# Norms fused into the feed-forwards, a delta rule with stacked fp32r parts, and grouped attention in two row halves

## The reference

```python
x = x + attn_causal_16_heads(norm(x))      # at1: head size 128
x = x + ffn_ternary(norm(x))               # ff2: silu(gate) * up, RMS norm, down; 1024 wide
x = x + delta_rule(norm(x))                # dr3: 16 heads of 16, 64 chunks of 16 tokens
x = x + ffn_ternary(norm(x))               # ff4
x = x + attn_grouped(norm(x))              # ga5: 32 query heads of 8, 8 key heads, not causal
x = x + ffn_hadamard(norm(x))              # ff6
x = x + attn_alibi_causal(norm(x))         # at7
x = x + ffn_hadamard(norm(x))              # ff8

# delta rule, per head, chunk by chunk (kc, vc: 16 x 16)
z = kc @ W
W = W - kc.T @ ((z - vc) * 2 / 256)
```

## Time and profile before

| | |
|---|---|
| median of 3 runs | 4026.34 us (4024.76 to 4029.02) |
| the profiled execution, its own time | 4044.84 us |
| its span | 4043.0 us |
| mean granted clock of TensorE | 0.955 |
| busy: PE, DVE, ACT, POOL | 3636.1, 2522.9, 1987.3, 762.7 us |

### The profile page before, as it was taken

How to read it: one execution, slowest core, us unless ns; L and a number is a source line. 1 busy time by engine, 2 the same in 40 slices (tenths; PEclk the granted TensorE clock), 3 DMA queues, 4 the chain that set the end, 5 groups by cost and what they waited for, 6 DMA issues and landing times. The chain is left out here.

```text
span 4043.0 us, 55040 instructions
## 1 busy us (share of the span) xinstructions
PE 3636.1 (90%) x19935; PEld 2559.5 (63%) x20020; DVE 2522.9 (62%) x4918; ACT 1987.3 (49%) x4137; POOL 762.7 (19%) x832
## 2 busy tenths in 40 slices
PE   6999999999387997867999999969799999999989
PEld 5878788787275986731333333248677777777767
DVE  5656566565653664537888888634576666666643
ACT  3555555554342332414777777722355555555532
POOL 1000000000131441310000000030144434444410
PEclk9999999999698997977999999989899999999999
DMA  1000000000000000011000000020000000000000
GB/s 51 11 7 11 11 5 11 11 5 2 32 1 20 1 0 3 1 44 44 20 16 17 17 16 17 1 80 1 22 8 11 11 5 11 11 7 9 2 32 22
DMA packets 32929, 61.42 MB, mean 15 GB/s; under 512 B 7186, under 2 KB 21522, under 8 KB 30842
## 3 DMA queue, kind: packets, MB, share of 16 engines
q1 hardware_dynamic: 32682, 58.12, 4.6%
HBM read 48.53 MB, written 9.18 MB: 14 GB/s over the span
## 5 line engine op out<-in xcount | busy, mean ns | idle before, releaser
L1495 DVE TENSOR_REDUCE ga5m_nm<-ga5m_M 128x1 f32<-128x1024 f32 x512 | 605.9, 1221 | 126.5 <-PE ga5m_M L1398 124.6
L1483 ACT ACTIVATE ga5m_pr<-ga5m_E 128x512 f32<-128x512 f32 x1024 | 558.5, 599 | 231.7 <-PE ga5m_E L1434 214.9
L376 PE MATMUL at_A<-at_pT,at_V 128*128 128x512 f32 (+3 forms) x1536 | 519.2, 488 | 7.4 <-issue 5.1
L319 POOL TENSOR_TENSOR at_prob<-at_prob,at_slope_row 128x128 f32<-128x128 f32 (+7 forms) x256 | 370.1, 1449 | 577.0 <-DVE at_prob L570 576.4
L376 PEld LDWEIGHTS at_A<-at_pT,at_V 128*128 128x128 f32 x1536 | 283.9, 190 | 248.7 <-issue 204.4
L464 ACT ACTIVATE at_pT<-at_T 128x512 f32<-128x512 f32 (+3 forms) x768 | 347.5, 488 | 107.2 <-PE at_T L417 105.9
L1398 PE MATMUL ga5m_M<-ga5m_K,ga5m_Q 128*128 128x512 bf16 x978 | 303.4, 389 | 61.4 <-DMA ga5m_Q<-in_zrows 38.9
L417 PE MATMUL at_T<-all_ident,at_prob 128*128 128x128 f32 x2304 | 336.4, 273 | 9.1 <-ACT at_pT L464 9.0
L1434 PE MATMUL ga5m_E<-ga5m_Q,ga5m_K 128*128 128x512 bf16 x986 | 336.1, 382 | 4.1 <-ACT ga5m_pr L1483 2.6
L1434 PEld LDWEIGHTS ga5m_E<-ga5m_Q,ga5m_K 128*128 128x128 bf16 x1024 | 98.9, 97 | 302.8 <-ACT ga5m_pr L1483 221.5
L417 PEld LDWEIGHTS at_T<-all_ident,at_prob 128*128 128x128 f32 x2304 | 268.1, 140 | 31.7 <-issue 8.9
(11 more groups left out here) (289 smaller groups left out, 8523.9 us busy)
## 6 DMA issues: line engine op xcount, KB each, us to landing
ga5m_Q<-ga_qs SPq DMA_DIRECT2D x96, 96.0 KB
at_raw_qk<-in_pqk SPq DMA_DIRECT2D x32, 256.0 KB, 2.8
at_raw_v<-in_pv SPq DMA_DIRECT2D x16, 256.0 KB, 3.1
at_raw_o<-in_po SPq DMA_DIRECT2D x32, 128.0 KB, 2.0
ga_qs<-ga5s_part SPq DMA_DIRECT2D x6, 512.0 KB
ga5m_K<-ga_ks SPq DMA_DIRECT2D x48, 48.0 KB
all_X<-in_x SPq DMA_DIRECT2D x1, 2048.0 KB
tq_raw<-in_gu SPq DMA_DIRECT2D x1, 2048.0 KB, 8.0
```

The lines of the kernel that those rows point to most:

```text
L319: nc.gpsimd.tensor_tensor(dst[:, 0:end], dst[:, 0:end], slope_row[n // 2 % 2][:, 0:end], ALU.add).then_inc(ramp_done, 1)
L376: mm = nc.tensor.matmul(bank[:, lo:GQ * P], V[b][:, kt, col:col + DH], pT[g][:, kt, lo:GQ * P], start=(kt == 0), stop=(kt == GQ * (g + 1) ...
L1483: nc.scalar.activation(pr[e % NR][:, :], Eb[e % 3][:, :], ACT.Exp, scale=scale).then_inc(e_done, 1)
L1495: nc.vector.tensor_reduce(nm[half % 2][:, m:m + 1], Mb[v % 2][:, :], AX.X, ALU.max, negate=True).then_inc(m_free[v % 2], 1)
```

## The change

Three parts. **Norms**: ff2, ff4 and ff6 also make the norm of the layer behind them (`nxt`), group by group as x is finished, so that `layer_norm` ahead of dr3, ga5 and at7 goes; the weights of dr3 and ga5 are fetched during ff2 and ff4 (`fetch`). **Delta rule**: one block dr3p makes rotary keys, values and turned keys, splits both into two fp32r parts and stores them; the stacks `KS` and `KVS`, which hold on 48 rows (3 x 16) high, low, high against high, high, low of one chunk, are read back from HBM by DMA, so that a product contracts over a chunk alone, in fp32r, and `MK` and its 256 ACT operations go. **Grouped attention**: two fp32r parts in place of three bf16 ones, stacks of 32 + 2 rows, held twice, in partitions 0 to 63 and 64 to 127. The two matmuls of an M use one half each, and successive E alternate between them.

```diff
 # normed_swiglu
+        if fetch:
+            @block.sync
+            def _(sp):
+                for tile, source, sem in fetch:
+                    sp.dma_start(tile, source).then_inc(sem, 16)
...
                     gate_up(g, f)
+                    if nxt is not None and f == 0 and g >= 2:
+                        turn_next(g - 2)
...
+            if nxt is not None:
+                turn_next(NG - 2)
             down(NG - 1, 0)
...
-                    if f == 0 and g:
+                    if f == 1 and g:
                         inverse(g - 1)
+                if nxt is not None and f == 5 and g:
+                    next_root(g - 1)
...
 # delta_rule
+        def load_stacks(sp, t, b):
+            rows = slice((b * QT + t) * P, (b * QT + t + 1) * P)
+            for i in range(3):
+                part = kvs[i == 1][rows, 0:D].rearrange("(j s) n -> s j n", s=C)
+                sp.dma_start(KS[b][C * i:C * i + C, :, :].bitcast(F32), part).then_inc(s_in[b], 16)
+                part = kvs[i == 2][rows, :].rearrange("(j s) n -> s j n", s=C)
...
+                for t in range(1, QT):
+                    for b in range(BATCH):
+                        sp.wait_ge(pp_done, (t - 1) * NP + (b + 1) * DC * PC)
+                        load_stacks(sp, t, b)
...
-                        mm = nc.tensor.matmul(PP[p % 2][:, e, :, :], MK[q % 2][:, 2 * pair + e, :],
-                                              KV[:, bass.ds(t + b * QT, 1), c, :, :].rearrange("p a v n -> p (a v n)"),
-                                              start=True, stop=True)
+                        mm = nc.tensor.matmul(PP[p % 2][:, e, :, :], KS[b][:, 2 * pair + e, c * P:(c + 1) * P],
+                                              KVS[b][:, 2 * pair + e, :, c, :], start=True, stop=True)
...
 # grouped_attention
-                    for lo in range(0, SEQ, 512):
-                        mm = nc.tensor.matmul(Mb[v % 2][:, lo:lo + 512], Q[n % NSLOT][:, x:x + P],
-                                              K[n % NSLOT][:, lo:lo + 512], start=True, stop=True)
+                    for half in range(2):
+                        lo = half * 512
+                        mm = nc.tensor.matmul(Mb[v % 2][:, lo:lo + 512], Q[n % NSLOT][rows(half), x:x + P],
+                                              K[n % NSLOT][rows(half), lo:lo + 512], start=True, stop=True)
...
-                    nc.tensor.matmul(Eb[e % 3][:, :], K[n % NSLOT][:, kt * P:(kt + 1) * P],
-                                     Q[n % NSLOT][:, x:x + 512], start=True, stop=True).then_inc(s_done, 1)
+                    nc.tensor.matmul(Eb[e % 3][:, :], K[n % NSLOT][rows(e % 2), kt * P:(kt + 1) * P],
+                                     Q[n % NSLOT][rows(e % 2), x:x + 512], start=True, stop=True
+                                     ).then_inc(s_done, 1)
```

More of the change, by code:

```diff
@@ L734, in turn @@
                         pe.wait_ge(ms_done, g - 1)
+                if nxt is not None and g >= 3:
+                    pe.wait_ge(next_done, (g - 2) * DC)
                 pe.wait_ge(xn_done, (g + 1) * GT)
@@ L774, in square_sums @@
                 pe.wait_ge(acc_done, (g + 1) * (FC - 1))
+                if nxt is not None and g:
+                    pe.wait_ge(next_done, g * DC)
                 if g + 1 < NG:
@@ L799, in _ @@
             down(NG - 1, 1)
+            if nxt is not None:
+                turn_next(NG - 1)
         @block.scalar
@@ L818, in high, with copy_next @@
                     nc.scalar.activation(sq[F % 2][:, :], hf[F % 2][:, :], ACT.Square).then_inc(sq_done, 1)
+            def copy_next(g):
+                for c in range(DC):
+                    act.wait_ge(nturn_done, g * DC + c + 1)
+                    nc.scalar.activation(nxt[0][:, c, g * N:(g + 1) * N], turned[c][:, :], ACT.Copy
+                                         ).then_inc(ncopy_done, 1)
             copy_turned(0)
@@ L828, in _ @@
                     high((F - 1) // FC, (F - 1) % FC)
+                if nxt is not None and f == 1 and g >= 2:
+                    copy_next(g - 2)
                 if f == 5 and g + 1 < NG:
@@ L946, in _ @@
                     low(F - 1)
+                if nxt is not None and len(nxt) == 2 and f == 1 and g >= 2:
+                    next_low(g - 2)
                 if f == 1 and g and rms:
@@ L959, in _ @@
                         low_turned(g + 1)
+                if nxt is not None and g:
+                    if f in (4, 5):
+                        next_measure(g - 1, range(2 * f - 8, 2 * f - 6))
+                    if f == 5:
+                        next_shifted(g - 1)
+                    if f in (6, 7):
+                        next_normalise(g - 1, range(2 * f - 12, 2 * f - 10))
             low(NF - 1)
+            if nxt is not None and len(nxt) == 2:
+                next_low(NG - 2)
             if rms:
@@ L1244, in grouped_attention @@
                 N = 2048
-                rem = [s.sb(f"rem{i}", [P, N]) for i in range(3)]
-                part = [s.sb(f"part{i}", [P, 3, N], BF16) for i in range(3)]
-                cast_done, rem_done, stored = s.sem("cast"), s.sem("rem"), s.sem("stored")
+                part = [s.sb(f"part{i}", [P, 2, N], F32R) for i in range(3)]
+                high_done, low_done, stored = s.sem("high"), s.sem("low"), s.sem("stored")
                 block = s.block()
@@ L1342, in _ @@
             def _(sp):
-                for i in range(NSLOT):
-                    sp.dma_start(K[i][NSTACK:P, :], io["krows"]).then_inc(fixed_in, 16)
                 def load(n):
@@ L1489, in _ @@
             def _(dve):
-                for i in range(NSLOT):
-                    nc.vector.memset(Q[i][64:P, :], 0.0).then_inc(zero_done, 1)
+                nc.vector.memset(Q[0][NSTACK:NSTACK + 32, :].bitcast(F32), 0.0).then_inc(ready[0], 1)
                 def maximum(v, tile):
```

451 lines of the change are left out of this document (309 added, 142 removed).

## The result

The changed kernel takes 4057.0 us (median of 5; 4056.6 to 4073.2) against 4026.2 before: ratio 1.0082 (1.0067 to 1.0098), slower by 0.8%, where 3960 and a gain were predicted. The profiled execution took 4056.55 us.

What follows compares the result with a forecast made beforehand. PE was taken to bound both the delta rule's loop and grouped attention. Terms -26.5 - 7.5 (early weights) - 9 + 43 + 11 - 77 = -66 from 4026.3 gave 3960 us; range 3850 to 4010, likeliest case 3925 to 3995.

Steps and rivals of the forecast that it cites:

- Norms, -26.5: Norms made inside ff2, ff4 and ff6: -47 for shorter gaps, +20.7 for work moved into their groups.
- nine us in place of 25.5: Gap behind ff2, with four of 16 tiles left there: 9 us for 25.5, so -16.5; same behind ff4.
- The step of the loop: Delta rule's loop at granted clock 0.50: 4.28 us a step for 3.51, +43 over 56 steps.
- The last tile changes by nothing: Delta rule's last tile, where only chains run: no change from its 22.0 us at clock 0.50.
- The first products: Delta rule's first 16 products, fp32r for float32: 13.8 us for 18.0, -4.2.
- the chain to the first product: Ahead of the delta rule's first product: split, 256 KB store and six stack loads, 9.5 us in all.
- The first reason given for the low clock, the entry: The reload stalls PE right ahead of the delta loop, so it is entered at the low level, 0.50.
- the other reason in the same sentence: The change halves PE's work on products, which made the delta loop's seven tiles unlike the last one.
- the fast case: Rival: delta loop at full clock, 2.65 us a step bound by DVE, -48 for +43; 3869 us, chance 0.22 with paired halves.
- Split and reload, +11: Ahead of grouped attention: larger stores, more loads and memsets add 11 us to 38.0, within 6 to 17.
- Grouped attention's steps, -77: Grouped attention's 256 steps: mean 2.68 us for 2.98, as M's two matmuls run side by side; ends -110 and -45.
- the floor: Grouped attention's step: busy sums of PE 2.34, ACT 2.40, DVE 2.44 us, taken as 2.68 with gaps.

Runs made afterwards that it cites:

- norms_alone: Changed kernel with the delta rule and grouped attention of before, so only the norms are new; 4037.7 us, ratio 1.0026 to before.
- norms_turn_late: Changed kernel with the next layer's transposes moved from step 0 to step 3 of a later group, copies to step 4; 4039.2 us.
- blocks_all: Changed kernel with all three norms in blocks of their own, delta loop entered after idle matmuls and its products made twice; 3949.3 us.
- after: The changed kernel itself, as profiled; 4056.55 us in that execution, median 4057.0.
- before_again: The unchanged kernel profiled a second time; 4033.05 us, where its first profiled execution took 4044.8.
- delta_warm: Changed kernel with 14 idle matmuls ahead of the delta rule's first product and two behind each of the 16 first products; 4051.5 us.
- delta_twice_cold: Changed kernel with each delta-rule product's matmuls made twice, no idle matmuls added; 3967.4 us, ratio 0.9856 to before.
- grouped_full_rows: Changed kernel with every E of grouped attention on all 128 rows, M unchanged; 4224.0 us, ratio 1.0479 to before.
- delta_warm_stale: Changed kernel with idle matmuls ahead of the delta loop and later stacks not reloaded, so its output is wrong; 4047.9 us.
- norms_grouped: Changed kernel with the delta rule of before; norms and grouped attention new; 3998.8 us, ratio 0.9930 to before.

## Why the prediction was wrong

The time came out 97 us above the one predicted: 37 in the norms, 28 in the delta rule, 32 in grouped attention, each as its part alone measured against its terms.

**Norms, -26.5; measured +10.5** (norms_alone). The step that failed: "nine us in place of 25.5", and half of the moved DVE work hidden. In the changed kernel PE waits behind the last gate and up of ff2:

```profile
PE ff_turned L770 <- DVE ff_nxn L1017: 6.1, 1, 6.1
```

And the moved work lengthens the groups. The third group of ff2, in the windows of the changed kernel:

```profile
1135.70:1172.30 36.60, 29.43 (x153) 24.95 (x153) 21.98 (x50) 15.14 (x28) 12.28 (x11) 0.90 0.00 1
```

The same group of before took 27.7 us at a granted clock of 1.00. I had charged 2.85 us a group; the second group has 2.2 (29.9 for 27.7), the third 8.9, and part of that is the clock. I also costed the transposes by their own length alone, and not by what is queued behind them: sums of squares and the multiplication down. norms_turn_late shows that this order was 18 of the 37 us. For ff6 the term was right (-10.5 predicted, -11.5 read, -13 by blocks_all).

**Delta rule, +31 with all its stages; measured +59.** The step of the loop was right: 4.28 predicted at 0.50, 4.27 read:

```profile
1402.41 1.20 PE L1862 MATMUL dr3m_PP<-dr_KVS,dr_KS 128*128 128x256 f32 x4
...
1406.68 0.56 PE L1862 MATMUL dr3m_PP<-dr_KVS,dr_KS 128*128 128x256 f32 x1
```

"The last tile changes by nothing" failed: the profiled execution of before was the exception, so the last tile too lost the high clock, some 13 us (8 x (3.41 - 1.79), its steps in after and in before_again). The first products, 23.9 us for 13.8, missed by a load that the prediction has nowhere. DVE's mask for the takes, `hm`, is issued on SP's queue behind the twelve loads of stacks, and landed 17.1 us later:

```profile
1304.35 0.63 DVE L1896 COPY mid_cs<-all_ident 128x128 f32<-128x128 f32 x4 [27.32 <-DMA dr3m_hm<-in_hm]
1304.90 1.28 DVE L1901 TENSOR_TENSOR dr3m_AB<-dr3m_PP,dr3m_hm 128x512 f32<-128x512 f32 x2
1305.64 1.39 PE L1862 MATMUL dr3m_PP<-dr_KVS,dr_KS 128*128 128x256 f32 x4 [10.75 <-DVE dr3m_AB L1901]
```

PE stood for 10.75 us after the first two products; the fourteen behind it took 12.0 us although at 0.50, so the low clock, which the term left out, cost little here. No run moves that load ahead. And the chain to the first product took 18 us, not 9.5:

```profile
L1862 PE MATMUL dr3m_PP<-dr_KVS,dr_KS 128*128 128x256 f32 x1 | 0.6, 580 | 18.0 <-DMA dr_KVS<-dr_kvl 18.0
```

(PE's groups of 1275 to 1294 us: the first product's idle time.) The rate was wrong there. The 380 GB/s of the earlier trace rows came from two loads, of 2 and 1 MB (the prediction says three of 1 MB); the stacks, in rows of 1 and 2 KB on 16 partitions each, came at 122 with the DMA engines busy throughout:

```profile
1282.00:1293.60 11.60, 0.00 (x0) 0.00 (x0) 0.00 (x0) 0.00 (x0) 0.00 (x0) 0.50 1.05 122
```

The first reason given for the low clock, the entry, is shown wrong by delta_warm and delta_twice_cold together; the other reason in the same sentence, that the change takes away the work that made the tiles with products unlike the last one, is what the runs bear out. That it was read off the last tile was in part luck: in three other executions that tile ran at 1.00.

For the fast case, DVE was to bound the step at 2.65; delta_warm ran at 2.26, what PE needs by the prediction's own sum (2.24). Adding the durations of DVE's operations overstates what it needs: its 24 operations in the second window of delta_warm add up to 10.2 us by the earlier trace rows, and it did them in 9.00, busy for 8.27.

**Split and reload, +11; measured +16**, inside its range. All but 1.5 us of it is in the stores: from the first split to the block of the reload 37.5 us (1859.0 to 1896.5) for 21.5 (1805.0 to 1826.5). They moved 425 GB/s from 1870 to 1882 us, but 215 in the 14.5 us behind, at half the DMA share, which the prediction's one rate of 380 doesn't have. The memsets and first loads took 18.3 us for 16.8.

**Grouped attention's steps, -77; measured -43.** That the halves run side by side was right. The step that failed is the floor: I compared sums of busy time of three engines (2.34, 2.40, 2.44) and took 2.68 for the mean step; the plain steps came to the ring through three E banks, 2.61, and the mean to 2.80 (2.97 before). I had added 0.24 to the busiest engine for everything else; the two steps of eight with turns add 0.19 to the mean over the ring alone.

The Trainium skill (TensorE: Matmul & The Clock Gate, Part 3, Packing small matmuls) says that matmuls in distinct row groups run concurrently; the trace agrees, two in 0.50 us. The Trainium skill (TensorEngine Tiling (Array Packing), Tiling Modes) says that a change of tiling mode drains TensorE; grouped_full_rows fits that, at some 0.2 us a change. The Trainium skill (TensorE: Matmul & The Clock Gate, Part 1) says that activity releases the throttle; delta_twice_cold agrees, while delta_warm_stale, with PE busy for 192 of 198 us, was not released.

## What to carry to other kernels

Before taking work off TensorE in a loop with short dependent matmuls, look for a stretch of the same kernel that already runs without that work and read its granted clock, in more than one execution: here the last tile hinted at it in one of four. The loop and last tile with cheaper products took 58 us more, and making those products twice gave 90 to 92 back. A floor for a loop is the longest ring through its buffers, with each engine's order in it, before it is any engine's sum of busy time. Price a moved instruction by what is queued behind it on its engine, not by its own length, and look what a small load is queued behind: a mask of 128 KB held PE for 10.75 us.

## What the runs showed of the hardware

Fewer matmul passes can lower the granted clock of a stretch in which PE is busy without a gap to speak of (0.50 in 198 us, PE busy 192); the high level was lost there with no pause above 1.33 us, though delta_warm stood through one of that length. The same loop with its products made twice rose from 0.50 by itself and held 1.00 through pauses of 1.10 us (delta_twice_cold). The last tile of the old loop ran at 0.50 in the first profiled execution and at 1.00 in three others (before_again, norms_alone, norms_grouped), 10.5 us apart from first to last Z: a term that rests on one profile's clock can be off by as much.

Loads in rows of 1 and 2 KB onto 16 partitions moved 122 GB/s with the DMA share at 1.05, where loads of 2 and 1 MB had moved 380.

A change between 64 and 128 rows cost TensorE some 0.2 us, and two fp32r matmuls in different row halves started together and took 0.50 us for both.
